# First inverse transform for two channels at a time, and two buffers for the shifted rows of the heads stage

## The reference, cut to what matters

```
xf = jnp.fft.fft2(x)
qf = xf.reshape(b, HEADS, hd, h * w)
...                                   # attn_f: 16x16 per head, from the l2-normed spectrum
out_cplx = jnp.einsum('bhcd,bhdn->bhcn', attn_f, qf)
out_f = jnp.abs(jnp.fft.ifft2(out_cplx)).reshape(b, c, h, w)
g = ...                               # two 1x1 convolutions of xf.real, batch norm, relu, sigmoid
out_f_l = jnp.abs(jnp.fft.ifft2(g * xf))
fsa = _conv(jnp.concatenate([out_f, out_f_l], axis=1), projf_w)
```

## Time and profile before

| | |
|---|---|
| Median of 3 runs | 28056.89 us (28052.81 to 28061.12) |
| Profiled execution, its own time | 28067.24 us |
| Its span, first to last instruction | 28065.3 us |
| Mean granted TensorE clock | 0.941 |
| PE busy | 24978.7 us (89%) |
| DVE busy | 19607.1 us (70%) |
| ACT busy | 13778.0 us (49%) |
| POOL busy | 12334.4 us (44%) |

### The profile page before, as it was taken

One profiled execution on the slowest core, in us unless ns is written; L12 is line 12 of the kernel. 1 busy time (PEld: TensorE's weight loads), 2 busy tenths in 40 slices (PEclk: granted clock), 3 DMA queues, 4 the chain that ended last, 5 costly groups with the idle time before them and its releaser, 6 DMA issues. The chain is left out here.

```text
span 28065.3 us, 339160 instructions
## 1 busy us (share of the span) xinstructions
PE 24978.7 (89%) x112751; PEld 14810.9 (53%) x112751; DVE 19607.1 (70%) x22312; ACT 13778.0 (49%) x19719; POOL 12334.4 (44%) x4613
## 2 busy tenths in 40 slices
PE   6988989989899899898988888888888888888888
PEld 4676766767767677576763333333333333333333
DVE  2462643625536255362569999999999999999999
ACT  1313213132141321412327777777777777777777
POOL 0000000000000000000019999999999999999998
PEclk7999989989899899998999999999999999999999
DMA  1121021110211202111124444444444444444444
GB/s 51 47 69 61 18 60 53 59 58 23 64 58 44 59 29 71 58 36 59 36 106 168 166 189 167 186 170 165 188 168 189 167 188 167 168 189 165 189 167 164
DMA packets 816296, 3112.35 MB, mean 111 GB/s; under 512 B 61866, under 2 KB 325435, under 8 KB 530363
## 3 DMA queue, kind: packets, MB, share of 16 engines
q1 hardware_dynamic: 815802, 3105.94, 29.8%
HBM read 2813.42 MB, written 292.30 MB: 111 GB/s over the span
## 5 line engine op out<-in xcount | busy, mean ns | idle before, releaser
L2110 POOL TENSOR_TENSOR hid<-hid,bc 128x2048 f32<-128x2048 f32 x2048 | 7810.9, 3814 | 931.8 <-DVE carry L2016 929.6
L1779 PE MATMUL yp<-hid,ident 128*128 128x512 f32 x16384 | 7354.5, 598 | 439.0 <-POOL hid L2110 439.0
L2084 POOL TENSOR_SCALAR_AFFINE_SELECT ident<-ident 128x128 f32<-128x128 f32 x1 | 0.3, 292 | 14546.4 <-DVE ident L1969 14546.4
L1779 PEld LDWEIGHTS yp<-hid,ident 128*128 128x128 f32 x16384 | 3042.8, 189 | 4644.0 <-issue 3959.5
L2002 DVE TENSOR_TENSOR_SCAN hid<-da,carry,t 128x512 f32<-128x512 f32 x3968 | 4858.1, 1266 | 111.1 <-DVE carry L2016 11.5
L2008 DVE TENSOR_TENSOR_SCAN hid<-t,carry,hid 128x512 f32<-128x512 f32 x3968 | 4828.6, 1259 | 27.9 <-ACT t L1850 27.2
L2103 POOL TENSOR_TENSOR hid<-bc,du 128x1024 f32<-128x1024 f32 x2048 | 4097.2, 2001 | 192.4 <-PE yp L1779 164.8
L1005 PE MATMUL bk<-region 128*128 128x256 f16 (+2 forms) x32688 | 3872.1, 276 | 24.1 <-ACT region L1302 19.2
L1005 PEld LDWEIGHTS bk<-region 128*128 128x128 f16 (+2 forms) x32688 | 3296.3, 116 | 622.9 <-issue 196.5
L1850 ACT ACTIVATE t<-delta,v_a 128x512 f32<-128x512 f32 x4096 | 2659.5, 681 | 1569.9 <-DVE hid L2008 1566.7
L1735 PE MATMUL pj<-xn,w_x 128*128 128x512 f32 x4096 | 2379.4, 735 | 1071.0 <-ACT xn L1875 1023.5
(11 more groups left out here) (248 smaller groups left out, 26585.4 us busy)
## 6 DMA issues: line engine op xcount, KB each, us to landing
bc<-bc_rows SPq DMA_DIRECT2D x1024, 2048.0 KB, 7.2
work<-in_shift_d SPq DMA_DIRECT2D x256, 512.0 KB, 3.6
xpad<-in_x SPq DMA_DIRECT2D x32, 2048.0 KB, 19.0
work<-in_x SPq DMA_DIRECT2D x128, 512.0 KB, 5.3
gated<-work SPq DMA_DIRECT2D x256, 256.0 KB, 2.3
region<-gated SPq DMA_DIRECT2D x256, 256.0 KB, 2.9
region<-heads SPq DMA_DIRECT2D x256, 256.0 KB, 3.1
region<-in_x SPq DMA_DIRECT2D x256, 256.0 KB, 3.6
```

Source lines behind the costliest of these rows:

```text
L1779: m = nc.tensor.matmul(yp[:, h, :], ident[:, :], hid[:, k % 4, n, :], start=False, stop=(g == G - 1 and n == 3), skip_group_check=True)
L2110: nc.gpsimd.tensor_tensor(hid[:, k % 4, :, :], hid[:, k % 4, :, :], bc[:, g, 1, :, :], ALU.mult).then_inc(s_hc.sem, 1)
```

## The change

In the inverse, frequency 64 is moved out of `XR` and `XI` into a tile of its own, `XLAST` (two times 128 channels). After the gates, its values are folded into frequency 0: the real parts' frequency 0 gets minus the imaginary part of 64, the imaginary parts' frequency 0 gets plus the real part of 64. Both were real lines of a real signal's transform, so after `inverse1` they stand apart again as real and imaginary part of one row, and `back` is given a row 0 that reads them so. With 64 frequencies per channel, two channels fit into the 128 columns of one stationary operand. `inverse1(p)` now handles 4 channels (two pairs) with four matmuls of the old width, 32 calls in place of 64; its output fills 128 partitions, channel 2q in the lower 64 and channel 2q+1 in the upper 64. ScalarE's `zcopy` copies 128 x 512 per call, 32 calls in place of 64. `inverse2(t)` reads 64 rows, the lower ones for even t, the upper ones for odd t, and so takes every other channel of 8; the store to DRAM (L955 before) takes channels in steps of two. The table `back` stands twice, one below the other.

What comes with it: the copy of each spectrum step is two instructions on each of ScalarE and VectorE (4 elements per partition into `XLAST`, 256 into `XR` or `XI`), the step from channel to channel in `XR` and `XI` is 64 elements, the last group of gates is 12 frequencies and four instructions of 128 elements are added on VectorE.

In the heads stage `shifted` has two buffers, and TensorE's order becomes shift(kk), turn(kk+1), mix(kk-1). ScalarE squares and roots kk-2 in step kk, VectorE adds kk-2. The loop is written by a new `rows_loop`: two steps ahead, 15 turns of two steps, two behind, and the last mix after it.

```diff
-        "back": np.concatenate([wt * cos[:HALF], wt * sin[:HALF]], 1),
+        "back": np.concatenate([back, back], 0),
...
+    wt = np.where(i[:64] == 0, 1.0, 2.0)[:, None] / HW
+    back = np.concatenate([wt * cos[:64], wt * sin[:64]], 1)
+    back[0, P:] = cos[64] / HW
...
-        XR = region[:, 0:P * HALF].rearrange("p (c u) -> p c u", u=HALF)
+        XR = region[:, 0:P * U64].rearrange("p (c u) -> p c u", u=U64)
+        XLAST = region[:, 2 * P * U64:2 * P * HALF].rearrange("p (i c) -> p i c", i=2)
...
-        shifted = wk(1024, 1024)
+        shifted = [wk(1024 + 2048 * i, 1024) for i in range(2)]
...
+        def rows_loop(eng, body):
+            body(0, 0)
+            body(1, 1)
+            with eng.Fori(1, NK // 2 - 1) as i:
+                body(i * 2, 0)
+                body(i * 2 + 1, 1)
+            body(NK - 2, 0)
+            body(NK - 1, 1)
...
-                    V.tensor_copy(XI[:, 4 * t:4 * t + 4, :], bk[4 + t % 2][:, 0:4 * HALF]...).then_inc(s_xi.sem, 1)
+                    spectrum = bk[4 + t % 2][:, 0:4 * HALF].rearrange("p (c u) -> p c u", u=HALF)
+                    V.tensor_copy(XLAST[:, 1, 4 * t:4 * t + 4], spectrum[:, :, U64])
+                    V.tensor_copy(XI[:, 4 * t:4 * t + 4, :], spectrum[:, :, 0:U64]).then_inc(s_xi.sem, 1)
...
+                    n_u = min(UG, U64 - g * UG)
+                    if n_u < UG:
+                        for i in range(2):
+                            V.tensor_tensor(XLAST[:, i, :], XLAST[:, i, :], gates[:, n_u, :], ALU.mult).then_inc(s_gx.sem, 1)
...
+                V.tensor_tensor(XR[:, :, 0], XR[:, :, 0], XLAST[:, 1, :], ALU.subtract).then_inc(s_gx.sem, 1)
+                V.tensor_tensor(XI[:, :, 0], XI[:, :, 0], XLAST[:, 0, :], ALU.add).then_inc(s_gx.sem, 1)
...
-                    for c in range(2):
-                        o = bk[p % 2][0:HALF, c * 256:(c + 1) * 256]
-                        mm(o, XR[:, 2 * p + c, :], k["cs"], start=True, stop=False)
-                        m = mm(o, XI[:, 2 * p + c, :], k["sc"], start=False, stop=True)
+                    for q in range(2):
+                        o = bk[p % 2][:, q * 256:(q + 1) * 256]
+                        mm(o, pairs[0][:, 2 * p + q, :], k["cs"], start=True, stop=False)
+                        m = mm(o, pairs[1][:, 2 * p + q, :], k["sc"], start=False, stop=True)
...
-                    mm(bk[2 + t % 2][:, :], k["back"][:, 0:P], Z[0:HALF, t % 2, :, 0:P], start=True, stop=False)
+                    r = slice(64 * (t % 2), 64 * (t % 2) + 64)
+                    mm(bk[2 + t % 2][:, :], k["back"][r, 0:P], Z[r, t // 2 % 2, :, 0:P], start=True, stop=False)
...
-                    if t + 1 < NK:
-                        inverse1(2 * t + 2)
-                        inverse1(2 * t + 3)
+                    if t + 2 < NK:
+                        inverse1(t + 2)
...
                     if not last:
                         turn(kk + 1)
-                    pe.wait_ge(s_shr.sem, s_shr.at(b, kk + 1))
-                    pe.wait_ge(s_shi.sem, s_shi.at(b, kk + 1))
+                    if not first:
+                        mix(kk - 1, 1 - par)
...
-                    act.wait_ge(s_o.sem, s_o.at(b, kk))
-                    cp(shifted[:, 0:512], bk[1][:, :]).then_inc(s_shr.sem, 1)
+                    act.wait_ge(s_o.sem, s_o.at(b, kk - 1))
+                    cp(shifted[par][:, 0:512], bk[1][:, :]).then_inc(s_shr.sem, 1)
```

More of the change, by code:

```diff
@@ L746, in add_squares, with body @@
                     V.tensor_tensor(sq2[0], sq2[0], sq2[1], ALU.add).then_inc(s_oa.sem, 1)
-                def body(kk, par, vrow):
-                    first = isinstance(kk, int) and kk == 0
+                def body(kk, par):
                     dve.wait_ge(s_sh.sem, s_sh.at(b, kk + 1))
-                    dve.wait_ge(s_o.sem, s_o.at(b, kk))
-                    V.tensor_copy(shifted[:, 512:], bk[2][:, :]).then_inc(s_shi.sem, 1)
-                    if not first:
-                        add_squares(kk - 1)
-                chunk_loop(dve, body)
+                    dve.wait_ge(s_o.sem, s_o.at(b, kk - 1))
+                    V.tensor_copy(shifted[par][:, 512:], bk[2][:, :]).then_inc(s_shi.sem, 1)
+                    if not (isinstance(kk, int) and kk < 2):
+                        add_squares(kk - 2)
+                rows_loop(dve, body)
+                add_squares(NK - 2)
                 add_squares(NK - 1)
@@ L1063, in _ @@
                     for u in us:
-                        m = mm(bk[6][:, i * P:(i + 1) * P], X[:, :, u], X[:, :, u], start=(u == us[0]), stop=(u == us[-1]))
+                        of_u = XLAST[:, i % 2, :] if u == U64 else X[:, :, u]
+                        m = mm(bk[6][:, i * P:(i + 1) * P], of_u, of_u, start=(u == us[0]), stop=(u == us[-1]))
                 m.then_inc(s_gram.sem, 1)
@@ L1129, in turn, with mix, body @@
                     m.then_inc(s_tr.sem, 1)
-                def body(kk, par, vrow):
-                    last = isinstance(kk, int) and kk == NK - 1
+                def mix(kk, par):
+                    pe.wait_ge(s_shr.sem, s_shr.at(b, kk + 1))
+                    pe.wait_ge(s_shi.sem, s_shi.at(b, kk + 1))
+                    pe.wait_ge(s_os.sem, s_os.at(b, 2 * kk - 2))
+                    o_re, o_im = bk[3 + 2 * par][:, :], bk[4 + 2 * par][:, :]
+                    re, im = shifted[par][:, 0:512], shifted[par][:, 512:]
+                    mm(o_re, mix_t[:, 0, :], re, start=True, stop=False)
+                    mm(o_re, mix_t[:, 2, :], im, start=False, stop=True)
+                    mm(o_im, mix_t[:, 0, :], im, start=True, stop=False)
+                    mm(o_im, mix_t[:, 1, :], re, start=False, stop=True).then_inc(s_o.sem, 1)
+                def body(kk, par):
+                    first, last = (isinstance(kk, int) and kk == i for i in (0, NK - 1))
                     pe.wait_ge(s_trc.sem, s_trc.at(b, kk + 1))
@@ L1315, in normalise, with xr_copy @@
                     cp(part, part, ACT.Identity, bias=col(5), scale=col(4)).then_inc(s_xn.sem, 1)
+                def xr_copy(t):
+                    act.wait_ge(s_s2.sem, s_s2.at(b, t + 1))
+                    spectrum = bk[2 + t % 2][:, 0:4 * HALF].rearrange("p (c u) -> p c u", u=HALF)
+                    cp(XLAST[:, 0, 4 * t:4 * t + 4], spectrum[:, :, U64])
+                    cp(XR[:, 4 * t:4 * t + 4, :], spectrum[:, :, 0:U64]).then_inc(s_xr.sem, 1)
                 for t in range(NK):
```

78 lines of the change are left out of this document (35 added, 43 removed).

## The result

The changed kernel takes 27679.22 us (median of 4 runs, 27676.24 to 27679.92), the kernel before 28056.71 us in the same series (28052.81 to 28061.12): a ratio of 0.9865, interval 0.9848 to 0.9882, or 377.5 us less. The forecast was 27603 us, within 27470 to 27770: the sign is right, the time lies in the range and 76 us above the forecast. The profiled executions are 27676.24 us after and 28067.24 us before, 391 us apart; the one of before lay 10.5 us above the median.

The account below looks back on a forecast made before the run. TensorE bounds the inverse by columns streamed; in the heads stage it waits for VectorE's copy. Inverse -351, heads -117, elsewhere +14 make -454 us: 28067.2 profiled becomes 27613, expected median 27603, range 27470 to 27770.

Parts of the forecast that it names:

- The inverse: Inverse stage: one of two inverse1 calls removed per step, small-tile price added; 3.80 us a step, 44 us less per image.
- The 0.35 us taken from the 25-row matmuls: Inverse: price per inverse2 of going to the small tile and back, read from matmuls with a 32x128 tile.
- the dear end: Inverse: twice the tile price, for four small-tile weight loads instead of two; only 33 us less per image, 262 in all.
- the rival with a free tile: Inverse and heads stage: tile change and ring cost nothing, steps of 3.45 and 5.93 us, 27470 us; chance 0.08.
- The heads stage: Heads stage: step falls from 6.575 to 6.1 us, 14.7 us less per image, 117 us for 8.
- a ring between `take_rows` and `turn`: Heads stage: turn needs take_rows, ScalarE's next copy needs the turned rows; ScalarE waits some 0.27 us per step.
- the wait for VectorE's copy: Heads stage: TensorE's stop before each mix, 0.66 us each, 19.2 us for 29; claimed to go.
- Gram: Gram stage: frequency 64 read without a step, 4 records fall from 0.233 to about 0.11 us, 0.5 us less per image.
- The side on which the rival stood: Gram: loads at 256 bytes take twice as long, 0.467 us, +61 us per image, 28088 us, slower; chance 0.05.
- The argument against it: Gram: hidden-layer loads stepping 132 and VectorE's gates stepping 128 elements cost nothing extra; 16-byte lines make 260 and 256 alike.
- Added elsewhere: Spectrum +1.5 us, gates +0.8, gram -0.5: sum +1.8 us per image, 14 us for 8 (0 to 60).
- The gates' last group: Gates: added multiplications and folds less a shorter last group, 0.8 us per image (0.5 to 1.5), bare on the path.

Follow-up runs that it names:

- `full_tile`: Changed kernel with the second inverse transform over all 128 rows, using two table copies each zero in one half; 27588.6 us, ratio 0.9835.
- `heads_only`: Kernel before with only the heads-stage part of the change (two buffers for shifted rows, mix one step later); 27926.3 us, ratio 0.9957.
- `sqrt_kept`: Changed kernel with the square root's activation table loaded once per image ahead of the heads stage, none in the loop; 27556.6 us, ratio 0.9825.
- `stride65`: Changed kernel with channels in XR and XI 65 elements apart again and all 65 values copied; values not the reference's; 27577.8 us, ratio 0.9832.
- `split64`: Changed kernel with a constant table read without a step replacing one operand of gram's products for frequencies 1 to 63; 27556.2 us, one run.
- `alternate`: Changed kernel with 128-row second inverse, root table loaded once per image, XI moved 128 bytes, gram's XR and XI products alternating; 27433.7 us, ratio 0.9783.

## Why the prediction was right or wrong

**The inverse: right in mechanism and in size.** Forecast -44 us per image and 3.80 us a step, measured -44.2 (mean of 8) and 3.84. The 0.35 us taken from the 25-row matmuls was 0.40 here. The worry behind the dear end, that four weight loads of a small tile cost twice, did not come true, nor did the rival with a free tile. ScalarE never held TensorE up: between 4031 and 4155 us the one wait of TensorE is the first, 8.6 us for the gates. The Trainium skill, "TensorEngine Tiling", section Key Properties, says that changing the tiling mode drains TensorE. It gives no price, and the drain does not show as idle time here; but that a matmul with a tile of 64x128 between full ones pays, and the same one over all 128 rows doesn't, is what the changed kernel (3.84 us) and `full_tile` (3.44 us) show.

**The heads stage: right.** Forecast -14.7 us per image and 6.1 us a step with a ring between `take_rows` and `turn`; measured -15.1 (mean of 8) and 6.14, the wait for VectorE's copy gone and the two small waits there, 7.3 and 5.9 us. `heads_only` gives 122 us for the part by itself, 117 forecast. `sqrt_kept` shows that the ring is tied by ScalarE's time: without its 1.28 us both waits vanish and 5.66 is left.

**Gram: wrong, the step that failed.** "Gram: frequency 64 is now read without a step ... 0.5 us less" became 11.0 us more per image, 88 for 8. The half microsecond itself was about right: `stride65`, which reads frequency 64 without a step and the rest at 65, takes 60.5 us where the kernel before takes 60.9. What failed is that the new distance of 256 bytes was put at nothing. The side on which the rival stood was right, and its bound in the forecast, over 0.25 us per load, was passed with 0.2765, but its price of twice the time wasn't: it added 19%, and the kernel stayed faster. The argument against it compared the wrong things. The hidden layer's loads step by 132 elements, which isn't a multiple of 64, and VectorE's gates are one reader at a time. `split64` shows that one reader pays nothing at 256 bytes (0.220 us); the gram stage has two at a time. The rule on lines of 16 bytes from the Trainium skill, "SBUF — State Buffer", note on cachelines, which makes steps of 260 and 256 bytes alike, doesn't cover this: here the measurement decides, 0.2765 against 0.2327 for the same matmuls. A sum with both cases at hand would have had to give this rival far more than 0.05, and priced it below twice.

**Added elsewhere: somewhat too dear.** The spectrum stage of the third image grew by 0.2 us, and what comes ahead of gram by 0.5 on average over the 8 (146.5 and 147.0), 1.5 forecast: waits of TensorE for ScalarE were 6 times and 6.3 us there, beside 6 and 6.0 in the earlier trace rows, so the small copies lay in the gaps. The gates' last group grew by 0.4 of the 0.8; the two parts were shorter than the rows of 128 elements had it. The hidden layer and gates together vary from image to image, between 119.8 and 122.1 us before and between 120.7 and 122.6 after, and the third image's -1.3 is no measure: over the 8 the means are 120.9 and 121.9, +1.0 us. The traces don't say what moves them.

**The sum.** Per image, as means of 8: ahead of gram +0.5, gram +11.0, hidden layer and gates +1.0, inverse -44.2, heads -15.1, and from the heads stage's first store to the next image -2.2 (1073.9 and 1071.7, with the same code). Together -49.0 us, 392 for 8, which gives 27675 from the 28067 of the profiled execution; measured 27676. The forecast from that execution was 27613, 63 too low: the gram term accounts for 92 of that, and the 2.2 us behind the heads stage, which were not foreseen, give back 18. That part varies from 1069 to 1075 us over images and runs with no change in its code; why stays open. So the time fell in the range with a term missing: 92 us had room in the 167 between the forecast and its upper end, and a share of it was offset by chance.

## What to carry to other kernels

Where a layout changes the distance between the elements of an operand, ask who else reads with the same distance at the same moment: two readers at 256 bytes cost a fifth more here than at 260, while one alone paid nothing, and so did two that stood in different groups of 16 bytes. A matmul of fewer rows isn't cheaper when its neighbours are full ones; padding it with zeros to the common tile can be. And when a wait is taken out of a loop, look for the ring that is late next, since the next gain (here a table load in every step) lies on it.

## What the runs showed of the hardware that was not expected

- Float32 gram records of 128x128 with both operands stepped: 0.279 us at 64 elements, 0.234 at 65, 0.245 at 66, 0.234 at 68, 0.241 at 72; with one stepped operand 0.220 at 64 and 0.232 at 65, equal for the stationary and the moving one.
- At 64 elements a load is slow (382 to 395 ns) beside a matmul that streams a column of the same aligned group of four values, and takes 319 to 330 ns beside any other: 240 of 240 first loads at multiples of four in the changed kernel, and every first load in `alternate`.
- Neighbouring elements take 1.78/16 = 0.11 us per record in the heads stage, so a stepped operand takes two to two and a half times as long at any of these steps.
- Going from 128x128 to a 64x128 tile and back costs 0.40 us in a step of eight and four records, split evenly between the two changes. It is not idle time in the profile.
- A single activation table load in a loop of 6.14 us was worth 0.48 us of it, not its 1.28: TensorE is the bound from 5.66 on.
